# A gather of 64x64 mixing blocks: copies out of a resident table, or transfers addressed by the index

## The reference

```
h  = einsum('bct,bcd->bdt', x, cond_weights[index])        # per sequence: a 64x64 block mixes its 64 tokens
x  = x + FFN(h)                                            # silu(h W1 + b1) * (h W2 + b2), then W3, b3
y  = x W + (x A[index]) B[index]                           # low-rank adapter chosen by the index
x  = x + y W_org + sum over 8 experts of coeff * (y down) up    # coeff: softmax of a router on mean(y)
```

## Time and profile before

| | |
|---|---|
| runs | 1001.23 us median (1001.08 to 1001.4) |
| the profiled execution's own time | 999.71 us |
| its span in the trace | 998.0 us |
| TensorE busy | 989.2 us, 99% of the span |
| VectorE, ScalarE, GpSimd busy | 743.1, 391.3, 39.1 us |
| HBM read, written | 75.51 MB, 8.39 MB |

### The profile page before, as it was taken

One profiled execution on the slowest core, in us unless ns is written; L12 is line 12 of the kernel. 1 busy time (PEld: TensorE's weight loads), 2 busy tenths in 40 slices (PEclk: granted clock), 3 DMA queues, 4 the chain that ended last, 5 costly groups with the idle time before them and its releaser, 6 DMA issues.

```text
span 998.0 us, 12355 instructions
## 1 busy us (share of the span) xinstructions
PE 989.2 (99%) x4768; PEld 815.9 (82%) x4768; DVE 743.1 (74%) x578; ACT 391.3 (39%) x349; POOL 39.1 (4%) x65
## 2 busy tenths in 40 slices
PE   8999999999999999999999999999999999999997
PEld 7888888888887888888898888888888878888886
DVE  2977977998866889674436888789885859878641
ACT  7553653543344333331055544543433532424110
POOL 2600000000000000000100000000000000000011
PEclk9999999999999999999999999999999999999999
DMA  9022044034014001425211211521330230031012
GB/s 356 3 91 100 1 166 171 22 108 167 1 43 155 14 1 64 164 90 180 115 43 43 84 43 46 208 85 33 119 145 2 84 127 0 1 106 43 1 64 106
DMA packets 22986, 84.68 MB, mean 85 GB/s; under 512 B 2691, under 2 KB 6803, under 8 KB 17043
## 3 DMA queue, kind: packets, MB, share of 16 engines
q1 hardware_dynamic: 20450, 75.24, 20.8%
q0 software_dynamic: 2400, 8.41, 2.2%
q10 hardware_dynamic: 80, 0.26, 0.1%
HBM read 75.51 MB, written 8.39 MB: 84 GB/s over the span
## 4 chain that ended last, share of the span: by engine, by line
PE 98%; issue 1%; DMA 0%; POOLq 0%; DVE 0%; POOL 0%; SPq 0%
PE banks L653 31%; PE banks L654 31%; PE banks L655 31%; PE banks L749 3%; PE banks L714 2%; PE banks L732 1%; DMA cond_sb<-cond_t_in 0%; DVE r L1017 0%; PE banks L762 0%; POOLq L1166 0%; POOL out_t L631 0%; PE banks L778 0%; POOL mix L464 0%; PE banks L772 0%; SPq L469 0%
## 5 line engine op out<-in xcount | busy, mean ns | idle before, releaser
L653 PE MATMUL banks<-s_hi,t_hi 128*128 128x512 f32 x1360 | 531.7, 391 | 0.0
L654 PE MATMUL banks<-s_lo,t_hi 128*128 128x512 f32 x1360 | 529.5, 389 | 0.0
L655 PE MATMUL banks<-s_hi,t_lo 128*128 128x512 f32 x1360 | 529.2, 389 | 0.0
L653 PEld LDWEIGHTS banks<-s_hi,t_hi 128*128 128x128 f32 x1360 | 255.3, 188 | 56.6 <-issue 3.8
L655 PEld LDWEIGHTS banks<-s_hi,t_lo 128*128 128x128 f32 x1360 | 255.3, 188 | 53.2
L654 PEld LDWEIGHTS banks<-s_lo,t_hi 128*128 128x128 f32 x1360 | 255.3, 188 | 52.5
L1017 DVE TENSOR_TENSOR r<-banks,r 128x1024 f32<-128x1024 f32 x92 | 111.4, 1219 | 97.7 <-PE banks L655 93.1
L919 DVE TENSOR_TENSOR t_lo<-w,t_hi 128x1024 fp32r<-128x1024 f32 x132 | 156.5, 1218 | 5.1 <-ACT t_hi L849 5.1
L830 ACT CAST s_hi<-st 128x2048 fp32r<-128x2048 f32 x40 | 76.5, 1913 | 198.0 <-PE banks L655 145.7
L849 ACT CAST t_hi<-w 128x1024 fp32r<-128x1024 f32 x132 | 133.3, 1048 | 49.0 <-PE banks L655 48.9
L830 ACT CAST s_hi<-r 128x2048 fp32r<-128x2048 f32 x34 | 65.0, 1913 | 203.3 <-PE banks L655 178.2
(11 more groups left out here) (70 smaller groups left out, 356.4 us busy)
## 6 DMA issues: line engine op xcount, KB each, us to landing
w<-w_up_in SPq DMA_DIRECT2D x16, 1024.0 KB, 4.8
w<-w_base_in SPq DMA_DIRECT2D x10, 1024.0 KB, 4.7
w<-w_down_in SPq DMA_DIRECT2D x8, 1024.0 KB, 5.4
r<-x_t_in SPq DMA_DIRECT2D x8, 1024.0 KB, 6.2
w<-w_lin_in SPq DMA_DIRECT2D x8, 1024.0 KB, 5.1
out_t<-r POOLq DMA_DIRECT2D x16, 512.0 KB, 3.2
we<-w_expin_in SPq DMA_DIRECT2D x10, 512.0 KB, 4.6
st<-x_pairs_in SPq DMA_DIRECT2D x8, 512.0 KB, 6.4
```

What stands on the lines that cost most here:

```text
L653: pe.matmul(out, w_hi, x_hi, start=start, stop=False, skip_group_check=True)
L654: pe.matmul(out, w_hi, x_lo, start=False, stop=False, skip_group_check=True)
L655: return pe.matmul(out, w_lo, x_hi, start=False, stop=stop, skip_group_check=True)
```

## The change

The table of all sixteen blocks is no longer loaded. Each of the 32 blocks is fetched from HBM by its own DMA (64 partitions by 256 bytes) whose source address comes from the index: for the first half the lower blocks by ScalarE's queue and the upper ones by GpSimd's; for the second half all 16 by SP's, after the first half's mixing. VectorE has no part in it any more. The router's query weights get a tile of their own.

```diff
-        cond_sb = sb("cond_sb", [P, NCOND, S])
         mix = sb("mix", [P, PAIRS, P])
+        wq_sb = sb("wq_sb", [P, K * KEY])
...
-        wq_sb = cond_sb[:, :, :].rearrange("p n s -> p (n s)")
...
-        mix_made = [sem("mix_made0"), sem("mix_made1"), sem("mix_made2")]
+        mix_loaded = [sem(f"mix_loaded{c}") for c in range(PAIRS)]
+        mix_loaded_by_pool = [sem(f"mix_loaded_by_pool{c}") for c in range(PAIRS)]
...
-        def make_mixing(eng, copy, half, blocks):
-            with eng.Fori(0, PAIRS // 2) as i:
-                for parity, j in blocks:
-                    rows = slice(j * S, (j + 1) * S)
-                    v = eng.value_load(idx_sb[0:1, bass.ds(i * 4 + (half * BH + parity * 2 + j), 1)],
-                                       min_val=0, max_val=NCOND - 1)
-                    eng.wait_ge(cond_loaded, 32)
-                    copy(mix[rows, bass.ds(i * 2 + parity, 1), rows].rearrange("p a m -> p (a m)"),
-                         cond_sb[rows, bass.ds(v, 1), :].rearrange("p a m -> p (a m)")).then_inc(
-                        mix_made[j * (1 + parity)], 1)
+        def load_mixing(eng, h, parts, loaded):
+            for c in range(PAIRS):
+                for j in parts:
+                    at, rows = h * BH + 2 * c + j, slice(j * S, (j + 1) * S)
+                    v = eng.value_load(idx_sb[0:1, at:at + 1], min_val=0, max_val=NCOND - 1)
+                    eng.dma_start(mix[rows, c, rows], cond_t[v]).then_inc(loaded[c], 16)
...
-            sp.dma_start(cond_sb[S:P, :, :], cond_t).then_inc(cond_loaded, 16)
...
                     if kind == "up0" and h == 0:
-                        sp.wait_ge(mix_made[0], 2 * PAIRS)
-                        for parity in range(2):
-                            sp.wait_ge(mix_made[1 + parity], 2 * (PAIRS // 2))
-                        sp.dma_start(wq_sb, wq_t).then_inc(wq_loaded, 16)
+                        sp.dma_start(wq_sb[:, :], wq_t).then_inc(wq_loaded, 16)
+                        sp.wait_ge(mixed_full, PAIRS)
+                        load_mixing(sp, 1, (0, 1), mix_loaded)
...
         def pool_engine(pool):
             pool.wait_ge(idx_loaded, 16)
-            make_mixing(pool, pool.tensor_copy, 0, [(0, 0), (1, 0)])
+            load_mixing(pool, 0, (1,), mix_loaded_by_pool)
...
-            pool.wait_ge(mixed_full, PAIRS)
-            make_mixing(pool, pool.tensor_copy, 1, [(0, 0), (1, 0)])
-            pool.wait_ge(mix_made[0], 2 * PAIRS)
-            make_mixing(pool, pool.tensor_copy, 1, [(0, 1), (1, 1)])
-            for parity in range(2):
-                pool.wait_ge(mix_made[1 + parity], 2 * (PAIRS // 2))
...
             def mixing(h):
                 for c in range(PAIRS):
                     bank = 2 * (c % 4)
-                    pe.wait_ge(mix_made[0], h * PAIRS + c + 1)
-                    pe.wait_ge(mix_made[1 + c % 2], h * (PAIRS // 2) + c // 2 + 1)
+                    pe.wait_ge(mix_loaded[c], 48 * h + 16 * (1 - h))
+                    pe.wait_ge(mix_loaded_by_pool[c], 16)
...
         def scalar_engine(act):
-            act.dma_start(cond_sb[0:S, :, :], cond_t).then_inc(cond_loaded, 16)
             act.wait_ge(idx_loaded, 16)
-            make_mixing(act, act.copy, 0, [(1, 1)])
+            load_mixing(act, 0, (0,), mix_loaded)
...
-            dve.wait_ge(idx_loaded, 16)
-            make_mixing(dve, dve.tensor_copy, 0, [(0, 1)])
...
-        "cond_t": np.asarray(L0_cond_weights).transpose(1, 0, 2),
+        "cond_t": np.asarray(L0_cond_weights),
```

More of the change, by code:

```diff
@@ L309, in build @@
         idx_loaded = sem("idx_loaded")
-        cond_loaded = sem("cond_loaded")
         small_loaded = sem("small_loaded")
```

## The result

The changed kernel takes 1002.97 us (median of 16 runs, 1002.02 to 1004.26) against 1000.87 us for the kernel before in the same comparison (16 runs, 999.37 to 1001.81). The ratio is 1.0023, with a 95% interval of 1.0015 to 1.0031: slower by about 2.3 us (2.1 between the medians), inside the predicted range. The profiled execution took 1002.43 us, its span is 1000.8.

The account below looks back on a forecast made before the run. TensorE, never waiting once mixing begins, was taken as the bound. The first product would move from 22.82 to the later of 24.0 and 23.9, +1.2 us, taking 1001.23 to 1002.4, stated as 1002.5 us; range 1000.6 to 1004.7.

Parts of the forecast that it names:

- The bound and the place of the loss: TensorE, busy 989.2 of 998.0 us, waits only before its first work; only a shifted first product changes the total.
- Chain 2: ScalarE's start: eight issues and a table load put its first copy at 13.9, VectorE's low part ready at 23.9.
- A step: One index read plus DMA issue on ScalarE at the start: 0.82 + 0.45 = 1.27 us, last issue ending at 12.6.
- Rival C: ScalarE's issues are slow, 0.65 to 0.85 us each, low part ready at 25.5 to 27.1: 1003.9 to 1005.5; chance 0.13.
- drain of 1.4 us: Skill's 1380 ns beside ScalarE's table load, making the kernel some 2.5 us slower; the prediction rejected it and kept 1.28.
- Chain 1: TensorE's start: pair 0's blocks issued at 3.3 land 4.8 us later, mixing starts at 8.1, first product at 24.0.
- the contended row: Earlier trace's 5.4 us landing of GpSimd's small transfers beside saturated weights; the forecast went near it, to 4.8.
- The slow stretch: Start of mixing at TensorE's lower level, first 3.42 us with 16 records, costing 1.7 us; carried over unchanged.
- rival B: Longer gap before mixing keeps TensorE at the lower level longer, product at 24.9 to 25.7: 1003.3 to 1004.1; chance 0.24.
- The sum: First product moves from 22.82 to the later of 24.0 and 23.9, +1.2 us; median 1001.23 becomes 1002.4, said as 1002.5.
- "No change": Whole kernel's time stays within 0.2% (2.0 us) of before, leaning slow; chance 0.61, against 0.37 slower and 0.02 faster.

Follow-up runs that it names:

- e2_half2: Kernel before, with only the second half's blocks fetched by SP's transfers and GpSimd's 16 copies gone; ratio 0.9996 to the kernel before.
- e3: Changed kernel with four warm-up matmuls on the 64x64 corner in place of two; ratio 1.0020 to the kernel before.
- e7: Changed kernel with five warm-up matmuls on a 128x128 zero tile in place of two on a 64x64 corner; ratio 1.0004 to the kernel before.
- e1: Changed kernel, but SP issues x of pair 0, then holds the rest of its stream until pair 0's blocks land; ratio 1.0028 to the kernel before.
- e5: Changed kernel, but SP fetches pair 0's two blocks itself, between x of pair 0 and x of pair 1; ratio 1.0010 to the kernel before.
- e4: Kernel before with three warm-up matmuls on the 64x64 corner in place of two; ratio 0.9994 to the kernel before.
- e6: Changed kernel fetching only 16 of 64 rows of each first-half block; ScalarE's first transfer landed after 5.6 us against 6.0, no ratio given.
- e9: Changed kernel, pair 0's blocks on SP behind x of pairs 0 and 1, four whole-array warm-ups, ScalarE's table load at program start; 999.8 us, ratio 0.9993.

## Why the prediction was right or wrong

**The bound and the place of the loss: right.** TensorE has no wait behind the first product in any of the profiles of before and after; the loss of the first product (2.74 us) is that of the span (2.8). e2_half2 confirms that the second half's transfers cost nothing that can be measured; they took 1.28 us each, not 1.15, as an issue of 64 pieces took 477 ns instead of 332.

**Chain 2, ScalarE's issues and the table load: right but for one step, and it didn't decide.** A step took 1.2 us for 1.27, the issues ended at 12.0 for 12.6, and there was one table load, right before the copy. That the low part was ready at 24.1 for 23.9 is in part luck: the first copy began at 13.32 for 13.9, but from there it took 10.8 us and not 10.02 "all of it back to back", as the second copy waited 0.80 us for TensorE, which mixed late and slowly. The two chains are not independent. Rival C is out. No drain of 1.4 us shows behind the table load: 12.02 + 1.28 = 13.30, and the copy starts at 13.32.

**Chain 1, the landing: right in kind, too small.** It was priced at 4.8 us from 3.3, which is 8.1, by GpSimd's queue. Measured: GpSimd issues at 3.71 and lands after 5.3, at 9.0, so the contended row was the one to take in full, and its first issue began 0.65 us after ScalarE's (3.71 against 3.06, forecast 3.3 for both). ScalarE's queue had been bounded at 4.3 by the earlier trace rows, taken beside a single weight load; in the full stream it took 6.0, outside the bound, and it was the last to land. This term, 4.8 us for a landing that was 5.3 and 6.0, is the one that was mis-sized, and it is 1.0 us of the miss: mixing at 9.14, not at 8.1. The same two transfers took 5.8 and 5.6 us in e3, 6.1 and 6.1 in e7, so it isn't the scatter of one start. e1 and e5 show the cause, by landings of 2.0 to 2.3 us when the stream isn't there. The Trainium skill (DMA: Bandwidth & Descriptors, Issuing engines are not separate DMA queues) says that transfers from several engines share the same 16 DMA engines and save issue time only. This case agrees: the second and third queue didn't get the blocks around SP's stream.

**The slow stretch: 0.5 us longer in this profile, and not shown to be the change's doing.** The prediction carried it over unchanged; 15.94 us from the start of mixing to the product became 16.42. That looks like rival B at half its price, but no profile bears out B's reason: e3 and e4 leave no gap and are no better, and e6 with a gap of 3.9 us has nearly the shortest slow stretch of all. The first 64 records took 9.03 to 10.03 us in the seven kernels with a warm-up on the corner in which nothing else held them up, so 0.5 us between two single profiles is within the scatter. Where in mixing the pace doubles differs too: at about 10.3 before, 13.6 after, 12 in e5. What decides the moment inside the start is left open; that the old warm-up doesn't count, and one on the whole array does, is shown by e3 against e7.

**The sum.** The forecast was +1.3 us on the median; measured are +2.1 between the medians and +2.3 (1.5 to 3.1) by the ratio. The forecast of +1.2 for the first product and the +1.0 of the landing make 2.2, so the landing alone would be enough for the ratio; the profile's 2.8 has the 0.5 of the slow stretch on top, and both profiled executions lie below the medians of their kernels, the one before by 1.2 us (999.71 against 1000.87), the one after by 0.5. The range held the result because it was wide: the size of the change was forecast at little over half, and what came is the price of rival B without its cause. "No change" was named the likeliest reading at 0.61; the median came out at 1002.97, just inside that side, the ratio just outside it.

## What to carry to other kernels

Here a small transfer beside a saturated stream landed in 5 to 8 us, not in 2, from ScalarE's queue as from GpSimd's; replace a bulk load by small ones only where nothing waits for the first of them, or issue that one ahead of most of the stream (e5 and e9, at a price in x that comes later). In a kernel whose bound engine never waits, a change of its waits can act only in its first and last microseconds: look there at what comes second, third and fourth, since they stood within 1 to 2 us of each other here. Warm TensorE up on the whole array (some 1.9 us here), and check in the records that the pace has doubled before the real work begins.

## What the runs showed of the hardware

- The landing time of a 16 KB transfer grows with what is in flight: 2.0 to 2.3 us with nothing but x of pair 0 ahead (e1, e5), 2.5 to 3.4 with one 512 KB transfer more (e9), 5.7 to 6.9 from ScalarE's queue and 5.3 to 5.7 from GpSimd's in the full stream of the changed kernel, up to 7.9 in e1. With a quarter of the pieces it is still 4.5 to 5.6 (e6). The Trainium skill (DMA: Bandwidth & Descriptors, Latency and other measured facts) holds that the fixed cost is mostly memory latency, which rises from 0.2 to 2 us at high load; the direction agrees, the 4 us more here are about twice that. No run here tells a wait in memory from one in the DMA engines.
- 7 us of float32 matmuls on a 64x64 corner left TensorE at its lower level (1057 ns a record throughout); on the whole array the same kind of record fell from 1061 to 592 ns within 7.0 us (e3, e7).
- The clock column read 1.00 in every one of these stretches. Only the durations of the records show the level.
